# Gated cross-attention and feed-forward on one Trainium2 core: tiles taken batch by batch in a program written out step by step, with three batches' values folded in the odd steps

## The reference, cut to what matters

```python
# x (4, 2048, 512), context (4, 77, 384), 16 heads of 64
q = split_heads(layernorm(x) @ Wq)
k, v = split_heads(context @ Wk), split_heads(context @ Wv)
attn = softmax(einsum('bhid,bhjd->bhij', q, k) * 64 ** -0.5)
out = merge_heads(einsum('bhij,bhjd->bhid', attn, v)) @ Wo + bo
x = x + tanh(g_xattn) * out
x = x + tanh(g_ffn) * (layernorm(x) @ W[idx] + b[idx])
```

## Time and profile before

| | |
|---|---|
| median of 3 runs | 1047.05 us (1046.21 to 1048.41) |
| the profiled execution | span 1047.8 us, 21829 instructions |
| PE busy | 1029.6 us, 98% |
| DVE busy | 853.0 us, 81% |
| ACT busy | 744.7 us, 71% |
| POOL busy | 443.8 us, 42% |

### The profile page before, as it was taken

How to read it: one execution, slowest core, us unless ns; L and a number is a source line. 1 busy time by engine, 2 the same in 40 slices (tenths; PEclk the granted TensorE clock), 3 DMA queues, 4 the chain that set the end, 5 groups by cost and what they waited for, 6 DMA issues and landing times.

```text
span 1047.8 us, 21829 instructions
## 1 busy us (share of the span) xinstructions
PE 1029.6 (98%) x6065; PEld 588.2 (56%) x6065; DVE 853.0 (81%) x1802; ACT 744.7 (71%) x2712; POOL 443.8 (42%) x639
## 2 busy tenths in 40 slices
PE   8988899999999999999999999999999999999998
PEld 6634455555555555555555555555555555555555
DVE  4877988888888887888888887888888887888876
ACT  3588877767776777767776777767776777767762
POOL 1486443444333443444333443444333443444422
PEclk9999999999999999999999999999999999999999
DMA  8423476555666656655666656655666656655656
GB/s 307 99 37 98 94 127 141 126 112 119 135 138 138 136 126 133 134 114 115 133 139 138 136 125 134 134 115 114 133 139 138 137 123 135 136 114 114 133 113 141
DMA packets 383639, 135.02 MB, mean 129 GB/s; under 512 B 361728, under 2 KB 363316, under 8 KB 383540
## 3 DMA queue, kind: packets, MB, share of 16 engines
q1 hardware_dynamic: 383476, 134.09, 59.0%
q0 software_dynamic: 64, 0.00, 0.0%
HBM read 27.48 MB, written 16.78 MB: 42 GB/s over the span
## 4 chain that ended last, share of the span: by engine, by line
PE 91%; DVE 4%; DMA 2%; ACT 2%; issue 1%; SPq 0%; POOL 0%; DVEq 0%; ACTq 0%
PE banks L1397 82%; PE banks L1625 3%; PE banks L1427 1%; PE banks L1502 1%; PE banks L1438 1%; DMA work<-work 1%; ACT work L890 1%; PE banks L1510 1%; DMA fold_area<-in_L_xattn_Wv 1%; DVE work L450 1%; DVE vw_area L1098 1%; ACT vw_area L842 1%; PE banks L1491 1%; DVE fold_area L1109 0%; DVE work L1201 0%
## 5 line engine op out<-in xcount | busy, mean ns | idle before, releaser
L890 ACT ACTIVATE work<-banks,red,cst 128x77 f32<-128x77 f32 x1024 | 410.3, 431 | 83.9 <-DVE red L1192 83.4
L1397 PE MATMUL banks<-fold_area,work 128*128 128x456 f16 (+1 forms) x2304 | 405.4, 335 | 3.0 <-DMA work<-work 2.3
L1397 PE MATMUL banks<-vw_area,work 128*128 128x512 f16 x1674 | 373.1, 380 | 3.0 <-DMA work<-work 3.0
L1397 PEld LDWEIGHTS banks<-fold_area,work 128*128 128x128 f16 x2304 | 225.2, 98 | 171.6 <-DMA work<-work 3.1
L1397 PEld LDWEIGHTS banks<-vw_area,work 128*128 128x128 f16 x1674 | 164.0, 98 | 189.2 <-DMA work<-work 3.7
L450 DVE SCALAR_TENSOR_TENSOR work<-work 128x256 f16<-128x256 f32 (+3 forms) x443 | 240.9, 578 | 1.4 <-ACT work L799 0.6
L890 ACT ACTIVATION_READ_ACCUMULATOR work<-banks,red,cst 128x1 f32 x1024 | 224.8, 220 | 0.0
L1190 DVE TENSOR_REDUCE stats<-banks 128x6 f32<-128x462 f32 (+1 forms) x192 | 112.0, 583 | 103.9 <-PE banks L1397 103.7
L1397 PE MATMUL banks<-work 128*128 128x256 f16 x1302 | 162.4, 272 | 0.5 <-DVE work L1277 0.3
L1397 PEld LDWEIGHTS banks<-work 128*128 128x128 f16 x1302 | 126.8, 98 | 32.0 <-DVE work L1277 0.6
L734 POOL TENSOR_TENSOR stats<-stats,cst 128x1 f32<-128x1 f32 x64 | 12.5, 195 | 284.1 <-DVE stats L1226 284.1
(11 more groups left out here) (148 smaller groups left out, 819.4 us busy)
## 6 DMA issues: line engine op xcount, KB each, us to landing
work<-in_x SPq DMA_DIRECT2D x64, 256.0 KB, 2.8
out<-work SPq DMA_DIRECT2D x63, 256.0 KB, 2.2
work<-work SPq DMA_TRANSPOSE x253, 3.1
fold_area<-in_L_xattn_Wo SPq DMA_DIRECT2D x4, 512.0 KB, 9.6
work<-in_L_ffn_W SPq DMA_DIRECT2D x2, 1024.0 KB, 7.5
fold_area<-in_L_xattn_Wq SPq DMA_DIRECT2D x2, 1024.0 KB, 13.0
fold_area<-in_L_xattn_Wk SPq DMA_DIRECT2D x2, 768.0 KB, 12.4
fold_area<-in_L_xattn_Wv SPq DMA_DIRECT2D x2, 384.0 KB, 7.6
```

The costliest lines, as they stand in the source:

```text
L890: nc.scalar.activation(probs_of(place, place + 1), s_heads(m, k)[:, h - h0, :], ACT.Exp, bias=nmx[:, h:h + 1], scale=exp_scale, accum_out= ...
L1397: mm = nc.tensor.matmul(ps, lhs(l), rhs(r), start=first and n == 0, stop=last and n == 2, skip_group_check=onto)
```

## The change

1. Tiles are taken batch by batch (`rows_of`: batch n // 16), and every step is written out: no loop, no registers.
2. Only the 4 VALUE units of batch 0 stay in `VISITS`. The other 12 are issued at the end of steps 5, 7, 9 and 11 of each of the first three batches' 16 steps (`LATE_STEPS`, `late_unit`), for the batch after, into banks 6 and 7 (`LATE_PAIR`), behind a wait for the last sum taken from bank 7. ACT's `value_high` of it comes in the next step ahead of the first exponentials, DVE's `value_low` behind the first maxima. `product` number 1 in that step waits until the banks are read.
3. Folded values have two slots (`SLOTS`) instead of four; `wo_raw` and `vT`, which late units still need, get room of their own.
4. One VALUE unit and seven KEY units are staged for POOL; SP loads the first two tiles of x early and no longer waits for the last value fold.

```diff
         def steps(eng, step):
-            for n in range(FIRST):
-                step(0, n)
-            with eng.Fori(0, LOOPS) as o:
-                for n in range(RING):
-                    step(*tile(o, FIRST, n))
-            for n in range(FIRST + LOOPS * RING, NT + 2):
+            for n in range(NT + 2):
                 step(*tile(0, 0, n))
...
-        STAGED_VALUES = [3, 6, 9, 12, 14]
-        STAGED_KEYS = [3, 7, 11, 15, 19, 23, 30]
+        STAGED_VALUES = [3]
+        STAGED_KEYS = [4, 8, 12, 16, 20, 24, 28]
...
+        LATE_STEPS = (5, 7, 9, 11)
+        LATE_PAIR = 6
+        def late_unit(o, m):
+            n = number(o, m)
+            at = n % NQ
+            return FOURS * (n // NQ + 1) + LATE_STEPS.index(at) if at in LATE_STEPS and n // NQ + 1 < B else None
...
             for n in range(2):
                 rows = slice(n * KT // 2, (n + 1) * KT // 2)
                 sp.dma_start(wq_raw[:, rows, :], wq.rearrange("(k p) n -> p k n", p=P)[:, rows, :]).then_inc(wq_loaded[n], 16)
-            sp.dma_start(xr[:, 0, :], x[0, 0:P, :]).then_inc(x_loaded[0], 16)
+            for n in range(2):
+                sp.dma_start(xr[:, n, :], x[0, n * P:(n + 1) * P, :]).then_inc(x_loaded[n], 16)
...
-            sp.wait_ge(v_folded, 4 * VALUES)
-            sp.dma_start(xr[:, 1, :], x[1, 0:P, :]).then_inc(x_loaded[1], 16)
             sp.wait_ge(bo_set, 16 * 2 * B)
             turn_x(0, 0)
...
ACT, step:
+                folded = late_unit(*tile(o, m, -1))
+                if folded is not None:
+                    value_high(folded)
                 if valid(o):
                     exponentials(o, m, 0)
...
DVE, step:
                 if valid(o):
                     maxima(o, m, 0)
+                folded = late_unit(*tile(o, m, -1))
+                if folded is not None:
+                    value_low(folded)
                 if grouped:
                     group_low_of(*pair, 2 if even else 0)
...
PE, product and the end of step:
+                folded = late_unit(*tile(o, m, 3))
+                if i == 1 and folded is not None:
+                    pe.wait_ge(vw_lo, highs_after(folded))
...
                 if multiplied and not even:
                     product(*begun, 6)
+                if late_unit(o, m) is not None:
+                    pe.wait_ge(f_added, nth_pair(*begun, PRODUCTS) + 6)
+                    value_unit(late_unit(o, m))
```

More of the change, by code:

```diff
@@ L69, in flamingo_layer @@
     PRODUCTS = 7
-    assert B == 4 and D == 512 and len(BANKS) == 3 and (NT - 2 - FIRST) % RING == 0
+    assert B == 4 and D == 512 and len(BANKS) == 3 and NT % RING == 0 and NQ % 2 == 0
     with ExitStack() as stack:
@@ L105, in flamingo_layer @@
         assert c.at <= 4 * A_WORDS
[L109 to L114, removed]
+        SLOTS = 2
+        MAIN_WORDS = SLOTS * 2 * MAIN * D // 2
+        SIDE_WORDS = KT * B * SIDE // 2
+        vw_area = sb("vw_area", [P, MAIN_WORDS + SIDE_WORDS + HP * D + HP * BJ])
+        c = Carve(vw_area)
+        vw = c.take(MAIN_WORDS).bitcast(F16).rearrange("p (b s c n) -> p b s c n", b=SLOTS, s=2, c=MAIN)
+        vw_side = c.take(SIDE_WORDS).bitcast(F16).rearrange("p (t b c n) -> p t b c n", t=KT, b=B, c=4)
+        wo_raw = c.take(HP * D).rearrange("p (h n) -> p h n", h=HP)
+        vT = c.take(HP * BJ).rearrange("p (h n) -> p h n", h=HP)
+        assert SIDE_WORDS <= MAIN_WORDS // SLOTS
+        sides = vw_area[:, MAIN_WORDS // SLOTS:MAIN_WORDS // SLOTS + SIDE_WORDS].bitcast(F16).rearrange("p (t b n) -> p t b n", t=KT, b=B)
         work = sb("work", [P, 16592])
@@ L367, in flamingo_layer @@
                   (SPREAD, 0), (TURN, 0), (REMAINDER, 2), (VALUE, 2), (REMAINDER, 3), (KEY, 0), (KEY, 1), (VALUE, 3), (TURN, 1),
[L368 to L373 removed]
+                  (KEY, 2), (KEY, 3), (KEY, 4), (KEY, 5), (TURN, 2), (KEY, 6), (KEY, 7),
+                  (KEY, 8), (KEY, 9), (TURN, 3)]
+        VISITS += [(KEY, v) for v in range(10, UNITS)]
         assert [n for kind, n in VISITS if kind == KEY] == list(range(UNITS))
[L376 removed]
+        ZEROED = (10, 11)
+        assert sorted(ROUND[VISITS.index((KEY, v)) % len(ROUND)] for v in ZEROED) == [0, 2]
+        assert VISITS.index((KEY, ZEROED[0])) > VISITS.index((TURN, HP // 2 - 1))
         def place_of(kind, n=0):
@@ L828, in value_high @@
             def value_high(n):
-                first = pair_of(VALUE, n)
+                first = value_pair(n)
                 act.wait_ge(v_folded, 4 * (n + 1))
-                if n >= VALUES - FOURS:
-                    act.wait_ge(side_turned, 16 * KT)
                 if staged(n):
```

38 lines of the change are left out of this document (17 added, 21 removed).

## The result

| | before | after |
|---|---|---|
| median of 20 runs each, us | 1048.20 (1046.21 to 1050.76) | 1049.74 (1047.12 to 1052.10) |
| ratio after / before | | 1.0015, 95% interval 1.0008 to 1.0022 |
| profiled execution: span, own time, mean clock | 1047.8, not at hand, 0.997 | 1045.6, 1047.8, 0.998 |

The changed kernel is slower by 1.5 us, 0.15%: within the 0.2% that was named as no change, and outside the predicted range, whose upper end was 1048.8. The forecast's base was the median of 3 runs, 1047.05; over 20 runs it is 1048.20. The profiled span fell by 2.2 us, nearly the predicted 2.3, but that is luck: it is one execution of each kernel, and the experiments show why it can't be read so.

A forecast was written before the change was run, and what follows sets the result against it. PE was taken as the bound, never idle in the steps and narrowly leading in the prologue. Terms -16.2 + 13.9 = -2.3 us took the span from 1047.8 to 1045.5, less 0.75 for the median: 1044.8, range 1042.0 to 1048.8.

The forecast's parts named there:

- The base: Time of the whole kernel before, from which the forecast was counted: 1047.05 us.
- The prologue, 16.2: Before tile 0's scores: removing 12 VALUE units shortens PE's way by 16.2 us, bounds 13.5 and 17.5.
- some 1.9 us of remaining waits: PE, TURN unit to tile 0's scores: two query copies on DVE and 0.77 before the scores, in 24.2 us.
- The pace of KEY units and the VALUE slots: PE in the prologue: 0.64 us for each of 30 KEY units, 1.02 us for each VALUE unit removed.
- remaining wait: PE between the last KEY unit and tile 0's scores: 0.77 us, counted among the waits that stay.
- POOL and the feed-forward matrix (a, b): Possible last arrivals at the prologue's end: POOL's splits and the matrix load both hold by about 1 us.
- Rival 1: The prologue gains only 13.5 to 14.5 us as POOL, matrix or DVE arrives last: 1046.5 to 1047.5 us; chance 0.27.
- The steps, 13.9: PE in the steps: 12 late units at 1.16 us each cost 13.9 us, bounds 12.2 and 16.8; evictions free.
- The loop, 0: Pass boundaries of the steps: writing out gains PE nothing, though DVE stalls 3.0 us per pass.
- Rival 3: Pass boundaries: the written-out program gains on its own, 7 x 3.0 = 21 us, to 1024; chance 0.02.
- From the span to the median: Whole kernel: the median of the runs is 0.75 us below the profiled span, so 1045.5 becomes 1044.8.
- The worst case of the prediction: Whole kernel: no case has this name; the range's upper end was 1048.8 us, a unit of 1.5 us.

The follow-up runs named there:

- experiment 16: Changed kernel with last KEY units in banks 4 to 7, first late unit in step 1, waits filled, `scales` moved earlier: 1045.26 us, ratio 0.9974.
- experiment 13: Changed kernel with DVE's six `scales` operations moved from behind KEY 12 to behind VALUE 2: 1047.48 us, ratio 0.9998.
- experiment 11: Changed kernel with last KEY units in banks 4 to 7, first late unit in step 1, PE's waits filled: 1047.61 us, ratio 1.0005.
- experiments 14: Kernel before with PE's waits filled by products nobody reads, and its steps written out: 1047.58 us.
- 15: Kernel before with PE's waits filled by products nobody reads, still a loop: 1046.89 us, ratio 0.9989.
- experiment 1: Kernel before, unchanged, run once more: 1047.87 us, ratio 0.9995.
- experiments 2: Kernel before with its steps written out and nothing else: 1049.61 us, ratio 1.0012.
- 3: Kernel before, written out, with tiles taken batch by batch and all 16 VALUE units in the prologue: 1047.99 us, ratio 1.0011.
- experiment 4: Changed kernel without its 12 late VALUE units and their evictions, all batches using batch 0's values: 1036.75 us, ratio 0.9900.
- experiment 5: Changed kernel, unchanged, run once more: 1051.86 us, ratio 1.0018.
- experiments 6: Changed kernel with 13 instead of 8 idle transposes at PE's start: 1049.07 us, ratio 1.0005.
- experiment 9: Changed kernel with PE's waits filled by products nobody reads and 13 transposes at the start: 1049.10 us, ratio 1.0013.
- 10: Kernel before with PE's waits filled by products nobody reads and 13 transposes at the start: 1047.14 us, ratio 0.9993.
- 7: Changed kernel with the last two KEY units moved to banks 4 to 7 and KEY 11 staged instead of KEY 12: 1050.44 us, ratio 1.0018.
- experiment 12: Changed kernel with each late unit's products computed twice: 1059.65 us, ratio 1.0107.

## Why the prediction was wrong

By its own steps, in its order:

- **The base.** 1047.05 was the median of 3 runs, and 1048.20 is that of 20: 1.2 of the 4.9 us between 1044.8 and 1049.74 are the base's.
- **The prologue, 16.2: the step that failed.** It gave 13.2, below its lower bound of 13.5. From the TURN unit to the scores of tile 0 PE took 27.3 us (49.59 to 76.86) and not 24.2, and the term in it that was too small is "some 1.9 us of remaining waits": they came to 4.4 (0.29, 0.72, 1.58 and 1.77). The pace of KEY units and the VALUE slots were right: without two hindrances the stretch took 23.8 us (49.70 to 73.48, experiment 16), and the gain was 16.4. The first was DVE's `scales`, which moved in time (by the VALUE units removed ahead of it) onto a POOL subtraction: 1.9 us (43.2 to 41.3, experiment 13). The prediction did ask what becomes the last arrival, but only among the large operations; these six had cost 0.14 to 0.16 each and weren't looked at. The second was the "remaining wait" of 0.77 ahead of the scores, taken over although the last KEY units change banks with the list: it became 1.77. Moving them away gave 1.4 alone (43.2 to 41.7, experiment 11), and both edits together 3.2 (to 40.0).
- **POOL and the feed-forward matrix (a, b): right**. The matrix was issued at 65.96 and took 5.2 us, so it was there at 71.2, well before ACT wanted it. POOL had 0.3 us to spare: its sixth split ended at 74.23 instead of 73, the scale of tile 1 was there at 75.42, ACT's normalization began at 75.72 right behind its last key copy, and its feed-forward copy followed at 77.11. Rival 1, a smaller gain of the prologue, came true in kind, though the gain is just under its 13.5 and the time above its 1047.5; and of the three it named as last arrival it was DVE, by six operations that nobody had looked at. ACT's rows:

```profile
75.72 0.81 ACT L799 ACTIVATE work<-work,stats 128x512 f32<-128x512 f32 x1
76.57 0.63 ACT L806 ACTIVATE work<-work 128x512 f16<-128x512 f32 x1
77.11 1.32 ACT L962 ACTIVATE work<-work,red 128x512 f16<-128x512 f32 x2
```

- **The steps, 13.9: right**, 13.5 measured (12 x 1.13). The split was nearly right too: 1.02 for the slot, 0.09 ahead of it, and 0.02 instead of 0.05 for the rest. That all evictions are free in the steps, and PE never waits, is what the windows show. The prediction's estimate from the Trainium skill, "TensorE: Matmul & The Clock Gate", section ④ DRAIN, was 0.96 a unit or 11.5 in all; the trace has 1.13, so the slot was the better witness.
- **The loop, 0: off by 0.7 in the median**, towards slower (experiments 14, 15); in the steps PE's pairs take 29.45 us either way. Rival 3, a gain of 21 us, is excluded.
- **From the span to the median: failed.** "The median of the runs is 0.75 below the profiled span" took one execution for a constant. By the runs' own records the time is 1.8 us above the span in every kernel made from before and 2.2 in every one made from after. The profiled run of before was one of its longer ones (experiment 1), with two half-clock stretches, and the +0.4 outside the span was in no term. Its cause is open: writing out and the order of tiles don't bring it (experiments 2 and 3 have 1.8), the late units neither (experiment 4 has 2.2); the new places of buffers and the early x loads weren't tried apart.
- **The clock: in no term.** Of 139 runs of the kernel before 73% have a mean clock of 0.998 or more, of 32 of the changed one 28%. At a mean clock of 1.000 they are at 1046.7 (38 runs) and 1047.2 (4 runs), so 0.5 apart; the medians over all are 1.9 apart, 1048.0 and 1049.9. The other 1.4 go with the clock: over the runs of both, a mean clock lower by 0.001 goes with a time longer by 0.9 to 1.0 us. That the low clock itself costs as much isn't shown, and the recorded mean misses some stretches (experiment 5). The worst case of the prediction had no place for this.

**The sum as it now stands**, at full clock: -13.2 + 13.5 + 0.7 (written out) + 0.4 (outside the span) = 1.4, of which the faster way from the scores of tile 0 to those of tile 4 gives back 0.9 (50.2 against 51.1 us in the traces, with three instead of four waits for transfers; at full clock 49.6 against 50.5, experiments 6 and 3): 0.5, as measured. The terms are each from one or a few traces, between the filled kernels' traces the last one is only 0.3 (49.8 against 50.1, experiments 9 and 10), and such agreement is partly luck.

**What stays open.** Why the changed kernel draws low-clock runs more often isn't settled. That waits of PE bring them is borne out by filling: it raised the mean clock in both kernels, to 1.000 in all runs of experiments 14 and 15 and in 11 of 12 of experiment 16. Against it as the whole account: experiment 9 filled the changed kernel as well and stayed at 0.9986 and 1049.1; experiment 13 took a wait of 1.6 us away and left the clock at 0.9968; and a wait of 3.0 us ahead of tile 1's attention was followed by half the clock in the changed kernel's trace and by the full one in those of experiments 4 and 6, so a wait alone doesn't decide it. A rival wasn't tried: in two of the traces with a low mean clock (experiment 5, 0.997, and 7, 0.993) the first value weights came late too, so that the projection began at 10.9 us instead of 9.7, and late transfers may both lengthen a run and open the waits. Nor is it known what writing out costs 0.7 for.

## What to carry over

When work is taken out ahead of a small operation, look at what the small operation now runs beside, and in a list that decides banks by position, at which banks the last entries take. A term worked out from slots of the trace holds well (1.16 against 1.13 per unit, 16.2 against 16.4), but the sum needs every hindrance at the new place, and most of a small difference (here 1.4 of 1.9 us) can go with how often the clock falls, which one profiled execution doesn't show. For a change of 0.2%, profile both kernels several times before a span is taken as the base.

## What the runs showed of the hardware beyond that

- A DVE operation with two SBUF inputs of one number per partition took 1.59 us instead of 0.16 beside a POOL subtraction, and ended with it. Six small DVE operations that took 0.5 us from first to last in the kernel before took 2.25 in the changed one, and cost PE 1.9 us (experiment 13).
- A 64x64 unit in 32 bits among 16-bit products of the full array costs 1.13 us of PE; a second one right behind it costs 0.86 (experiment 12).
- Filling PE's waits with products that nobody reads made the kernel before 1.1 us faster (1046.89 against 1047.96, ratio 0.9989, 0.9978 to 0.9999) without touching its work.
- A half-clock stretch that made one attention 1.46 us longer cost 0.6 us of the way, as a later wait for a transfer was gone.
